# Plain stores of the shared output and a shifted loop start: a gated-expert block on one Trainium2 core

## The chip, the core and the metric

The kernel runs on one core of a Trainium2 chip. The metric is the device time of one execution in microseconds (us). Matmuls run on TensorE (PE); VectorE (DVE), ScalarE (ACT) and GpSimd (POOL) do the elementwise work; SyncE (SP) issues nearly all transfers, and each engine runs its own instruction stream, kept in step by semaphores.

## The reference

Eight rows (sequences) of 512 tokens by 256 channels go through two layers, both with a residual:

```python
# layer 0: routed experts (top 2 of 8 per row) and one shared expert
rw = softmax(cond_8); w, sel = top_k(rw, 2); w = w / w.sum(-1)
mlp(x, g, u, d) = (gelu(x @ g) * (x @ u)) @ d        # 256 -> 1024 -> 256
x = x + sum_k w[b, k] * mlp(x, skill[sel[b, k]]) + mlp(x, shared)
# layer 1: a linear map plus LoRA experts weighted by cond_8
x = x + x @ W_base.T + b_base + 2 * sum_e cond_8[b, e] * (x @ As[e].T) @ Bs[e].T
```

All of it is float32.

## The kernel before

Every float32 operand is split in two parts of a format that TensorE multiplies in one pass: ScalarE rounds it ("hi", `take_hi`, L1201), VectorE subtracts to get the rest ("lo", `take_lo`, L1586). A product is three passes, hi*hi, hi*lo and lo*hi (`product`, L851 to L855), so TensorE's work is one long list of 128x128 by 512 (or 256) matmuls. Larger products are done with seven block products in place of eight; the sums of weight blocks that this needs are made by GpSimd (four operations, L806 to L811), split by ScalarE and VectorE, and the results are put together by VectorE (L1648, L1650, L1885, L1900, L1902) and GpSimd (`c22`, L739, and `ex_c22`, L820).

**Shared part (0 to about 255 us).** Four quarters `q` of two rows each; each has four units `u`, a unit being one fourth of the inner channels: gate and up products, then the down products of the unit before, added up in four PSUM banks `acc[0..1][0..1]`. When a quarter is done, ScalarE copies `acc[0]` (`acc0_to_stage`, L1308) and VectorE `acc[1]` (`acc1_to_stage`, L1689) to `stage`. In HBM there are two scratch tensors of rows, `xt_dram` and `base_dram`; SyncE stores the transposed tokens to both (`store_xt`, L503). GpSimd then issues two transfers that add `stage` to `base_dram` (`add_shared`, L706 and L709) and signal `sh_stored`. `stage` is also where GpSimd makes its sums of tokens (`t_a`, `t_b`, L770 and L782; `t_c` lies in `post`), the sums of the first rows (`sums_of_x`, L746) and, in rows, the sums of weights (`s_tmp`), so each of these waits for `sh_stored`. In the unit loop GpSimd's order is: c22 of gate, t_a, c22 of up, t_b, t_c.

**Rows (about 255 us to the end).** Eight rows `b` of K = 16 steps `k`, two experts of eight chunks. Steps come in pairs; pairs 1, 3, 5, 6, 7 (`SEVEN`, in row 0 without 1) are done as seven products on the last even step, pairs 0, 2, 4 as whole products, with VectorE's multiply of gate and up at L1976. In step 1 of row b+1 VectorE adds `base` and the PSUM sums of row b (`layer1_sum`, L1842), and in step 5 TensorE does layer 1 of row b (`layer1`, 24 matmuls in PSUM banks called ps_acc). `base` is loaded by SyncE once per row (L629 for row 0, L659 later) when layer 1 of the row before has let it go. Each engine has its own loop over rows 1 to 6, two rows an iteration, three iterations (GpSimd: one row an iteration). TensorE's loop starts at step `TURN_STEP` = 6 of row 1; VectorE's, ScalarE's and SyncE's start at step 0 of row 1 (VectorE L2018), so they turn at the starts of rows 3 and 5.

In row 0, GpSimd first does `add_shared(Q - 1)`, waits for `sh_stored` = 16 * B, and makes the weight sums of pair 3 (`sums_of_weights(b, 1, True)`, L828); ScalarE splits them in step 5 and VectorE too (`SUMS_FIRST`), VectorE behind its multiply of step 5; TensorE needs them in the second of the seven products of step 6.

**Start.** TensorE does 13 filling transposes of the identity (L975), turns the first row (L969), does 5 more fillers (L981), and begins the first gate (`first_gate`, L874 to L883).

## Time and profile before

| | |
|---|---|
| median of 3 runs | 806.21 us (804.76 to 808.38) |
| profiled execution | 809.66 us, its span 807.8 us |
| TensorE busy | 793.7 us, 98% of the span, 4282 matmuls |
| VectorE busy | 655.3 us, 81% |
| ScalarE busy | 498.3 us, 62% |
| GpSimd busy | 313.4 us, 39% |
| granted TensorE clock, mean | 0.995 |
| moved by DMA | 108.82 MB |

The span is from the first to the last instruction of the profiled execution; the time of an execution has some 1.9 us around it. Ends of matmuls are modelled, so a stretch of matmuls that is drawn longer than the same list elsewhere is also a loss, beside the gaps. "Idle before, releaser" is the time for which an engine stood still before an instruction and what ended it; "issue" there means that the profile shows nothing that it waited for.

### The profile page before, as it was taken

The numbers are of one execution on the slowest core, as the hardware profiler recorded it, in microseconds if no ns is written. First come the engines' busy times: TensorE is split into PE (matmuls) and PEld (weight loads), VectorE is DVE, ScalarE is ACT, GpSimd is POOL, SyncE is SP. The second block draws the span as 40 slices with busy tenths as digits, with TensorE's granted clock in tenths as the row PEclk, the third lists the DMA queues.
The fourth block names the chain that finished last, engine by engine and source line by source line (L and its number), as shares of the span: only waits on it lengthen the run. The fifth ranks groups of instructions, "written<-read, shape, count | busy, mean of one in ns | idle before, by whom it ended". The sixth has DMA issues, their size and how long they took to land.

```text
span 807.8 us, 14151 instructions
## 1 busy us (share of the span) xinstructions
PE 793.7 (98%) x4282; PEld 690.3 (85%) x4282; DVE 655.3 (81%) x872; ACT 498.3 (62%) x808; POOL 313.4 (39%) x308
## 2 busy tenths in 40 slices
PE   9999999999999899999999999999999999999998
PEld 8888878878878789889888978988988998898897
DVE  4866888988987578978987977897888789789777
ACT  5554554555664466666766766676766767667663
POOL 1531431521530245435444424633445352454341
PEclk9999999999999999999999999999999999999999
DMA  7456806708516632743463256265246526623400
GB/s 221 115 169 196 194 2 193 173 0 272 121 51 183 170 118 79 234 133 117 138 212 95 84 192 169 78 205 159 87 130 206 135 69 205 169 78 101 109 1 27
DMA packets 139894, 108.82 MB, mean 135 GB/s; under 512 B 63040, under 2 KB 131392, under 8 KB 139840
## 3 DMA queue, kind: packets, MB, share of 16 engines
q1 hardware_dynamic: 136384, 104.00, 41.9%
q0 software_dynamic: 3456, 4.19, 3.3%
q8 instruction: 22, 0.36, 0.2%
q14 instruction: 32, 0.26, 0.1%
HBM read 79.34 MB, written 28.84 MB: 134 GB/s over the span
## 4 chain that ended last, share of the span: by engine, by line
PE 87%; DVE 4%; issue 3%; POOL 2%; DMA 2%; ACT 1%; DVEq 0%; ACTq 0%; POOLq 0%
PE ps_ring L853 54%; PE ps_acc L853 31%; DMA base_scratch<-stage 2%; DVE inner_lo L1586 1%; DVE xc L1586 1%; DVE post L1675 1%; POOL stage L807 1%; PE ps_ring L975 0%; ACT wide L1201 0%; PE ps_acc L1072 0%; PE ps_acc L969 0%; DVE post L1976 0%; POOL stage L806 0%; POOL stage L811 0%; ACT inner_hi L1201 0%
## 5 line engine op out<-in xcount | busy, mean ns | idle before, releaser
L853 PE MATMUL ps_ring<-xc,wide 128*128 128x512 f32 (+1 forms) x1854 | 386.8, 357 | 3.0 <-DVE post L1648 3.0
L853 PEld LDWEIGHTS ps_ring<-xc,wide 128*128 128x128 f32 x1854 | 317.5, 189 | 56.7 <-DVE post L1648 4.7
L1201 ACT CAST inner_hi<-post 128x512 fp32r<-128x512 f32 x192 | 116.3, 621 | 97.8 <-DVE post L1976 30.7
L853 PE MATMUL ps_acc<-inner_hi,wide 128*128 128x512 f32 x504 | 166.3, 390 | 0.0
L1586 DVE TENSOR_TENSOR inner_lo<-post,inner_hi 128x512 fp32r<-128x512 f32 (+1 forms) x145 | 137.2, 955 | 3.0 <-ACT inner_hi L1201 2.6
L1204 ACT ACTIVATE post<-post 128x256 f32<-128x256 f32 (+1 forms) x114 | 62.2, 558 | 98.2 <-DVE post L1900 69.7
L820 POOL TENSOR_TENSOR post<-post 128x256 f32<-128x256 f32 x78 | 82.0, 1072 | 95.6 <-ACT post L1453 95.6
L853 PEld LDWEIGHTS ps_acc<-inner_hi,wide 128*128 128x128 f32 x504 | 94.8, 188 | 18.9
L853 PE MATMUL ps_acc<-inner_lo,wide 128*128 128x512 f32 x252 | 98.5, 391 | 0.0
L853 PE MATMUL ps_ring<-xc 128*128 128x256 f32 x576 | 80.7, 287 | 3.7 <-DVE xc L1586 3.6
L853 PE MATMUL ps_acc<-inner_hi,sh_dn 128*128 128x512 f32 x256 | 83.9, 389 | 0.0
L1204 ACT ACTIVATE post<-ps_ring 128x512 f32<-128x512 f32 (+1 forms) x117 | 61.6, 529 | 30.9 <-PE ps_ring L853 25.4
L853 PEld LDWEIGHTS ps_ring<-xc 128*128 128x128 f32 x576 | 75.2, 196 | 4.1 <-DVE xc L1586 3.8
L806 POOL TENSOR_TENSOR stage<-xbuf 128x256 f32<-128x256 f32 x24 | 19.7, 822 | 143.2 <-DVE xc L1586 131.8
L1586 DVE TENSOR_TENSOR wide<-raw,wide 128x1536 fp32r<-128x1536 f32 (+4 forms) x38 | 58.0, 1526 | 20.3 <-ACT wide L1201 19.7
L739 POOL TENSOR_TENSOR post<-post 128x512 f32<-128x512 f32 x24 | 34.2, 1424 | 97.9 <-DVE post L1650 97.9
L1863 DVE SCALAR_TENSOR_TENSOR post<-post,coef_now 128x256 f32<-128x256 f32 x78 | 51.9, 666 | 18.7 <-ACT post L1204 17.8
L1976 DVE SCALAR_TENSOR_TENSOR post<-post,coef_now,ps_ring 128x512 f32<-128x512 f32 x50 | 37.3, 746 | 31.9 <-PE ps_ring L853 23.2
L1586 DVE TENSOR_TENSOR xc<-stage,xc 128x1024 fp32r<-128x1024 f32 (+1 forms) x50 | 60.2, 1209 | 3.5 <-ACT xc L1201 3.5
L853 PEld LDWEIGHTS ps_acc<-inner_hi,sh_dn 128*128 128x128 f32 x256 | 48.0, 188 | 10.0
L853 PEld LDWEIGHTS ps_acc<-inner_lo,wide 128*128 128x128 f32 x252 | 47.5, 188 | 8.4
L1201 ACT CAST wide<-raw 128x1536 fp32r<-128x1536 f32 (+4 forms) x40 | 48.9, 1222 | 8.9 <-DMA raw<-in_L_cond_shared_up_dram 6.0
(130 smaller groups left out, 1074.8 us busy)
## 6 DMA issues: line engine op xcount, KB each, us to landing
rights_scratch<-xc SPq DMA_DIRECT2D x6, 1792.0 KB, 11.3
raw<-n_L_cond_skill_gate_dram SPq DMA_DIRECT2D x32, 256.0 KB, 2.8
raw<-in_L_cond_skill_up_dram SPq DMA_DIRECT2D x32, 256.0 KB, 3.4
raw<-n_L_cond_skill_down_dram SPq DMA_DIRECT2D x32, 256.0 KB, 3.8
xbuf<-n_L_cond_skill_gate_dram SPq DMA_DIRECT2D x32, 256.0 KB, 2.7
xbuf<-in_L_cond_skill_up_dram SPq DMA_DIRECT2D x32, 256.0 KB, 3.2
xbuf<-n_L_cond_skill_down_dram SPq DMA_DIRECT2D x32, 256.0 KB, 3.5
xt_scratch<-xbuf SPq DMA_DIRECT2D x8, 512.0 KB, 3.4
```

The lines of the kernel that those rows point to most:

```text
L739: G.tensor_tensor((g_t if part == GATE else i_t)[3], v57, u1, ALU.add).then_inc(c22_done, 1)
L806: G.tensor_tensor(s1, a21, a22, ALU.add).then_inc(ex_s1_made, 1)
L807: G.tensor_tensor(s3, a11, a21, ALU.subtract)
L820: last = G.tensor_tensor(ex_v[:, half], ex_v[:, half], ex_u1[:, half], ALU.add)
L853: last = pe.matmul(dst, left_[a], right_[b], start=start and n == 0, stop=stop and n == len(PASSES) - 1, skip_group_check=adds)
L1201: return nc.scalar.copy(dst, src)
L1204: return nc.scalar.activation(dst, src, ACT.Gelu_apprx_tanh)
L1586: return V.tensor_tensor(dst, src, hi.bitcast(F32), ALU.subtract)
L1675: V.tensor_tensor(i_t[t], g_t[t], i_t[t], ALU.mult).then_inc(sh_mul, 1)
L1863: V.scalar_tensor_tensor(out=to, in0=g, scalar=coef_now[:, par, s:s + 1], in1=up, op0=ALU.mult, op1=ALU.mult).then_inc(ex_mul, 1)
L1976: V.scalar_tensor_tensor(out=inner[k % 2], in0=gelu[k % 2], scalar=coef_now[:, par, s:s + 1], in1=ring[2 + k % 2][:], op0=ALU.mult, op1=AL ...
```

## The change

- `base_dram` is gone. `store_xt` stores the tokens once. A new `sh_dram` takes the shared output alone, by plain stores that SyncE issues (`store_shared`), for quarters 0 and 1 behind the first token store of the next iteration, for quarter 2 before the last store of rights, for quarter 3 in row 0 behind the loads of the layer 1 constants.
- SyncE loads `base` from `sh_dram`. GpSimd adds the tokens to it in SBUF with one accumulating transfer a row (`add_tokens`), issued behind `ex_c22(b, 1)`, which is the c22 of step 6. It signals `base_ready`, and VectorE's `layer1_sum` waits for that.
- VectorE's loop begins at step 8 (`DVE_TURN_STEP`) of row 1: `row` takes a range of steps; the turns lie in the middle of rows 3 and 5.
- The 5 filling transposes behind the first turning are left out.
- Counts of `xt_stored` are halved; a few waits on events of long before are added, and three operations in `layer1_constants` are cut in halves.

```diff
@@ -62,6 +62,8 @@
     X1_LO_STEP = 4
     TURN_STEP = 6
+
+    DVE_TURN_STEP = 8
@@ -124,8 +126,7 @@
         last_bank = [acc[1][0], acc[1][1], ring[0], ring[1]]
         xt_dram = nc.dram_tensor("xt_scratch", [B, P, HC * S], F32, kind="Internal").ap()
-
-        base_dram = nc.dram_tensor("base_scratch", [B, P, HC * S], F32, kind="Internal").ap()
+        sh_dram = nc.dram_tensor("sh_scratch", [B, P, HC * S], F32, kind="Internal").ap()
         rights_dram = nc.dram_tensor("rights_scratch", [B - 1, P, 2 * NP * HS], F32, kind="Internal").ap()
@@ -390,6 +391,7 @@
         t_made = sem("t_made")
         v_done = sem("v_done")
         c22_done = sem("c22_done")
+        base_ready = sem("base_ready")
         x_rows = x.rearrange("b (p t) h -> b p t h", t=TT)
         out_rows = out.rearrange("b (p t) h -> b p t h", t=TT)
@@ -498,9 +500,22 @@
                     sp.wait_ge(xt0_in, 2 * r + 2)
                 else:
                     sp.wait_ge(xt_in, 4 * (qn - 1) + 2 * r + 2)
-
-                for to in (xt_dram, base_dram):
-                    sp.dma_start(to[2 * qn + r], xbuf[:, r * 2 * S:(r + 1) * 2 * S]).then_inc(xt_stored[r], 16)
+                sp.dma_start(xt_dram[2 * qn + r], xbuf[:, r * 2 * S:(r + 1) * 2 * S]).then_inc(xt_stored[r], 16)
+
+            def shared_place(q, n):
+                if q == 0:
+                    return sh_dram[n], stage[:, n, :]
+
+                return (sh_dram[2 * q:2 * q + 2].rearrange("r p (m h t) -> p m h r t", m=HC, h=2)[:, :, n],
+                        stage[:, n, :].rearrange("p (m r t) -> p m r t", m=HC, r=2))
+
+            def store_shared(q):
+                sp.wait_ge(acc0_out, 2 * (q + 1))
+                to, what = shared_place(q, 0)
+                sp.dma_start(to, what).then_inc(sh_stored, 16)
+                sp.wait_ge(acc1_out, 2 * (q + 1))
+                to, what = shared_place(q, 1)
+                sp.dma_start(to, what).then_inc(sh_stored, 16)
             def store_rights(q):
@@ -571,6 +586,8 @@
                     sp.wait_ge(xt_in, 4 * q + 2)
                     load_x_blocks(2 * qn + 1, x_blk)
                 store_xt(qn, 0)
+                if q > 0:
+                    store_shared(q - 1)
                 if qn < Q - 1:
                     sp.wait_ge(xt_in, 4 * q + (2 if q == 0 else 4))
                     load_x_blocks(2 * qn + 2, x_blk)
@@ -590,11 +607,12 @@
             sp.wait_ge(right_ready, rights(Q - 1, NP))
             sp.wait_ge(right_hi, rights(Q - 1, NP))
             for r in range(2):
-                sp.wait_ge(xt_stored[r], 32 * Q)
+                sp.wait_ge(xt_stored[r], 16 * Q)
             sp.wait_ge(xt_in, 4 * (Q - 1))
             sp.dma_start(xf_first, xt_dram[0]).then_inc(x0_landed, 16)
             gate0, up0, down0 = first_expert()
             fill_slot(2, gate0, up0, down0)
+            store_shared(Q - 2)
             store_rights(Q - 1)
             sp.wait_ge(x_ready, 1)
@@ -626,7 +644,7 @@
                 if first:
                     sp.wait_ge(sh_mul, 4 * NU)
                     sp.wait_ge(sh_stored, 16 * (B - 2))
-                    sp.dma_start(base, base_dram[b]).then_inc(base_landed, 16)
+                    sp.dma_start(base, sh_dram[b]).then_inc(base_landed, 16)
                     sp.wait_ge(sh_inner_hi, 4 * NU)
                     sp.wait_ge(sh_inner_ready, 4 * NU)
@@ -639,6 +657,7 @@
                             .then_inc(layer1_landed, 16)
                     sp.dma_start(w_nat, w_base.rearrange("(c p) h -> p c h", p=P))\
                         .then_inc(layer1_landed, 16)
+                    store_shared(Q - 1)
                     sp.wait_ge(sums_stored, 16)
                     sp.wait_ge(sh_down_done, 2 * NU)
@@ -656,7 +675,7 @@
                     sp.wait_ge(x1_ready, b)
                     sp.wait_ge(sh_stored, 16 * B)
-                    sp.dma_start(base, base_dram[b]).then_inc(base_landed, 16)
+                    sp.dma_start(base, sh_dram[b]).then_inc(base_landed, 16)
                     load_routed(b, 1, range(3, 4))
                     if not last:
                         load_routed(b + 1, 0, range(0, 1))
@@ -690,24 +709,6 @@
             G.affine_select(out=ident[:], in_=ident[:], compare_op=ALU.not_equal, fill=1.0,
                             base=0, pattern=[[-1, P]], channel_multiplier=1).then_inc(ident_ready, 1)
-            def shared_place(q, n):
-                if q == 0:
-                    return base_dram[n], stage[:, n, :]
-
-                return (base_dram[2 * q:2 * q + 2].rearrange("r p (m h t) -> p m h r t", m=HC, h=2)[:, :, n],
-                        stage[:, n, :].rearrange("p (m r t) -> p m r t", m=HC, r=2))
-
-            def add_shared(q):
-
-                for r in range(2):
-                    pool.wait_ge(xt_stored[r], 32 * (q + 1))
-                pool.wait_ge(acc0_out, 2 * (q + 1))
-                to, what = shared_place(q, 0)
-                pool.dma_start(to, what, accum_op=ALU.add).then_inc(sh_stored, 16)
-                pool.wait_ge(acc1_out, 2 * (q + 1))
-                to, what = shared_place(q, 1)
-                pool.dma_start(to, what, accum_op=ALU.add).then_inc(sh_stored, 16)
-
             def left_sums(j):
                 v = raw[j % 2][:, 0:4 * PW].rearrange("p (g c i) -> p g c i", g=2, c=HC)
@@ -782,8 +783,6 @@
                     G.tensor_tensor(both(t_b), xh(1, 1), xh(0, 1), ALU.subtract).then_inc(t_made, 1)
                     pool.wait_ge(t_made, 4 * q + 1)
                     G.tensor_tensor(both(t_c), xh(1, 1), both(t_a), ALU.subtract).then_inc(t_made, 1)
-                if q > 0 and j == 0:
-                    add_shared(q - 1)
                 if u < PAIRS - 1:
                     pool.wait_ge(sh_landed[u + 1], 32)
@@ -820,9 +819,15 @@
                     last = G.tensor_tensor(ex_v[:, half], ex_v[:, half], ex_u1[:, half], ALU.add)
                 last.then_inc(ex_c22_done, 1)
+            def add_tokens(b):
+
+                pool.wait_ge(base_landed, b * 16 + 16)
+                pool.dma_start(base, xt_dram[b], accum_op=ALU.add).then_inc(base_ready, 16)
+
             def row(b, first, last):
                 if first:
-                    add_shared(Q - 1)
+                    for r in range(2):
+                        pool.wait_ge(xt_stored[r], 16 * Q)
                     pool.wait_ge(sh_stored, 16 * B)
                     sums_of_weights(b, 1, True)
@@ -831,6 +836,7 @@
                     ex_c22(b, 0)
                 sums_of_weights(b, 2)
                 ex_c22(b, 1)
+                add_tokens(b)
                 sums_of_weights(b, 3)
                 sums_of_weights(b, 4)
                 ex_c22(b, 2)
@@ -947,8 +953,8 @@
             def shared_down_part(u, p):
                 q, j = divmod(u, PAIRS)
-                if q == 0 and p == 0:
-                    pe.wait_ge(sh_dn_ready, j + 1)
+                if q == 0 or j == 0:
+                    pe.wait_ge(sh_dn_ready, j + 1 if q == 0 else PAIRS)
                 if u == 0 and p == 0:
                     pe.wait_ge(xt0_in, 4)
@@ -976,9 +982,6 @@
             pe.wait_ge(x_landed[0], 16)
             for c in range(HC):
                 turn(acc[0][c], x_nat, c)
-
-            for _ in range(5):
-                pe.transpose(ring[3][:, 0:P], ident[:], ident[:])
             first_unit()
             for u in range(1, NU):
@@ -1613,7 +1616,7 @@
                     dve.wait_ge(right_hi, rights(qn - 1, NP))
                     dve.wait_ge(right_ready, rights(qn - 1, NP))
-                dve.wait_ge(xt_stored[r], 32 * qn)
+                dve.wait_ge(xt_stored[r], 16 * qn)
                 blk = x_blk1 if qn == 1 and r == 1 else x_blk
                 for c in range(HC):
                     V.transpose(xt(r, c), blk[:, c, :]).then_inc(xt_in, 1)
@@ -1679,6 +1682,8 @@
                 take_lo(inner_s[1][:, t, :], i_t[t], inner_s[0][:, t, :]).then_inc(sh_inner_ready, 1)
             def acc1_to_stage(q):
+                if q > 0:
+                    dve.wait_ge(acc0_out, 2 * q)
                 dve.wait_ge(sh_down_done, 2 * PAIRS * (q + 1))
                 if q == 0:
@@ -1822,18 +1827,25 @@
             inner_part(NU - 1, 3)
             def layer1_constants():
+
+                dve.wait_ge(acc0_out, 2 * Q)
+                dve.wait_ge(layer1_landed, 6 * 16)
                 dve.wait_ge(a_hi, 1)
-                take_lo(a_s[1], a_nat, a_s[0]).then_inc(a_ready, 1)
+                for half in (slice(0, P), slice(P, H)):
+                    last = take_lo(a_s[1][:, half], a_nat[:, half], a_s[0][:, half])
+                last.then_inc(a_ready, 1)
                 dve.wait_ge(turned_w, 1)
                 V.tensor_copy(b_t[:], ps_misc[1][:, 0:H]).then_inc(b_t_done, 1)
-                V.tensor_copy(w_id[:], ps_misc[0][:]).then_inc(w_turned, 1)
+                for c in range(HC):
+                    last = V.tensor_copy(w_id[:, c * H:(c + 1) * H], ps_misc[0][:, c * H:(c + 1) * H])
+                last.then_inc(w_turned, 1)
                 dve.wait_ge(w_turned, 1)
                 for c in range(HC):
                     d = w_id[:, c * H + c * P:c * H + (c + 1) * P]
                     V.tensor_tensor(d, d, ident[:], ALU.add).then_inc(w_id_done, 1)
             def layer1_sum(b):
-                dve.wait_ge(base_landed, b * 16 + 16)
+                dve.wait_ge(base_ready, b * 16 + 16)
                 for m in range(HC):
                     if m < HC - 1:
                         dve.wait_ge(sum_done, b + 1)
@@ -1909,7 +1921,7 @@
                 ex_inner(par, s, inner[1].rearrange("p (t n) -> p t n", t=2),
                          gelu[1].rearrange("p (t n) -> p t n", t=2), ex_c2[:, :, HS:S])
-            def row(b, par, first, last):
+            def row(b, par, first, last, steps=range(K)):
                 split_at = SPLIT_FIRST if first else SPLIT_LATER
                 sums_at = SUMS_FIRST if first else SUMS_LATER
@@ -1935,7 +1947,7 @@
                     cols = slice(0, 2 * S) if first else slice(HS, S)
                     take_lo(x_cur(1 - par, 1)[:, cols], xf[:, cols], x_cur(1 - par, 0)[:, cols]).then_inc(x_ready, 1)
-                for k in range(K):
+                for k in steps:
                     s = k // IC
                     if k // 2 in sevens_of(first):
                         if k % 2 == 0:
@@ -2015,11 +2027,13 @@
                     .then_inc(x1_ready, 1)
             row(0, 0, True, False)
+            row(1, 1, False, False, range(DVE_TURN_STEP))
             with dve.Fori(0, (B - 2) // 2) as i:
-                row(i * 2 + 1, 1, False, False)
+                row(i * 2 + 1, 1, False, False, range(DVE_TURN_STEP, K))
                 row(i * 2 + 2, 0, False, False)
-            row(B - 1, 1, False, True)
-            dve.wait_ge(base_landed, B * 16)
+                row(i * 2 + 3, 1, False, False, range(DVE_TURN_STEP))
+            row(B - 1, 1, False, True, range(DVE_TURN_STEP, K))
+            dve.wait_ge(base_ready, B * 16)
             for c in range(HC):
                 if c == 0:
```

## Rows read from the trace of the kernel before

**Rows 1.** Waits of TensorE: us in total, times, longest.

```profile
PE ps_ring L853 <- DVE post L1648: 3.0, 4, 1.6
```

**Rows 2.** Timeline of TensorE: start, us, line, tiles, count, idle before.

```profile
103.92 0.97 PE L853 MATMUL ps_ring<-xc,wide 128*128 128x512 f32 x3 [1.61 <-DVE post L1648]
...
164.82 0.96 PE L853 MATMUL ps_ring<-xc,wide 128*128 128x512 f32 x3 [0.76 <-DVE post L1648]
...
279.79 0.87 PE L853 MATMUL ps_ring<-xc,wide 128*128 128x256 f32 x6
284.24 3.85 PE L853 MATMUL ps_ring<-xc 128*128 128x256 f32 x18 [3.58 <-DVE xc L1586]
...
290.08 0.40 PE L853 MATMUL ps_acc<-inner_hi,wide 128*128 128x512 f32 x1
```

**Rows 3.** Chain that ended last, in time order: start, us, what.

```profile
265.69 13.16 DMA base_scratch<-stage
...
414.11 5.44 PE ps_acc L853 x24
...
484.65 5.44 PE ps_acc L853 x24
490.09 5.03 PE ps_ring L853 x42
...
551.49 5.44 PE ps_acc L853 x24
...
619.57 5.44 PE ps_acc L853 x24
```

**Rows 4.** Window behind the wait of row 0: PE busy, PEclk, DMA share.

```profile
284.20:286.00 1.80, 1.76 (x8) 0.50 0.99 324
```

**Rows 5.** GpSimd: the tile base_scratch (ns min/median/max), then its timeline.

```profile
L709 POOL DMA_DIRECT2D base_scratch<-stage x4: 1182/1921/1992, 85.8 to 265.7; - x4
...
98.08 1.74 POOL L782 TENSOR_TENSOR stage<-xbuf 128x512 f32<-128x512 f32 x1
...
493.73 1.76 POOL L820 TENSOR_TENSOR post<-post 128x256 f32<-128x256 f32 x2 [2.85 <-ACT post L1453]
502.66 0.88 POOL L806 TENSOR_TENSOR stage<-xbuf 128x256 f32<-128x256 f32 x1 [7.16 <-DVE xc L1586]
```

**Rows 6.** Timeline of VectorE.

```profile
98.59 1.77 DVE L1675 TENSOR_TENSOR post<-post 128x512 f32<-128x512 f32 x1
...
101.99 0.68 DVE L1675 TENSOR_TENSOR post<-post 128x512 f32<-128x512 f32 x1
...
278.69 0.75 DVE L1976 SCALAR_TENSOR_TENSOR post<-post,coef_now,ps_ring 128x512 f32<-128x512 f32 x1 [1.68 <-PE ps_ring L853]
...
465.60 0.75 DVE L1976 SCALAR_TENSOR_TENSOR post<-post,coef_now,ps_ring 128x512 f32<-128x512 f32 x1 [1.71 <-PE ps_ring L853]
...
469.92 0.75 DVE L1976 SCALAR_TENSOR_TENSOR post<-post,coef_now,ps_ring 128x512 f32<-128x512 f32 x1 [2.05 <-issue]
...
500.70 0.75 DVE L1976 SCALAR_TENSOR_TENSOR post<-post,coef_now,ps_ring 128x512 f32<-128x512 f32 x1
...
504.16 0.75 DVE L1976 SCALAR_TENSOR_TENSOR post<-post,coef_now,ps_ring 128x512 f32<-128x512 f32 x1 [1.22 <-PE ps_ring L853]
```

**Rows 7.** Chain at the start of the kernel.

```profile
4.56 1.71 PE ps_acc L969 x8
6.26 1.07 PE ps_ring L981 x5
...
11.65 0.87 PE ps_acc L969 x8
```

**Rows 8.** Page, DMA issues: count, KB each, us to landing.

```profile
rights_scratch<-xc SPq DMA_DIRECT2D x6, 1792.0 KB, 11.3
...
xt_scratch<-xbuf SPq DMA_DIRECT2D x8, 512.0 KB, 3.4
```

**Rows 9.** Timeline of SyncE's queue, the base load of row 3.

```profile
484.08 0.34 SPq L659 DMA_DIRECT2D post<-base_scratch  x1
```

## The prediction

> **What bounds the kernel now.** I read the waits of TensorE first, then its own timeline around them, the chain of work in order of time for the distances between equal pieces, and last VectorE and GpSimd beside each gap. TensorE is busy 98% of the span, so anything that does not take a gap or an instruction from TensorE is worth nothing. The reader is to see that the gaps are few and that each has one owner [rows 1, 2]:
>
> - Four waits of 3.0 us together for VectorE's L1648 (the sum v57 of a shared matrix). The two longest, 1.61 and 0.76 us, stand in the second unit of the second and of the third quarter [rows 1, 2].
> - One of 3.58 us for the lo half of the weight sums, in step 6 of row 0 [rows 2]. Its real price is more: these seven products run from 279.79 to the next down product at 290.08, 10.29 us, where the same piece takes 5.03 elsewhere [rows 2, 3]. That is 5.26 us: the wait and a slow stretch behind it, in which the granted clock is 0.50 (1.2 of 2.4 GHz) [rows 4].
> - Something at the start of rows 3 and 5. The layer 1 blocks (24 matmuls, 5.44 us) lie 66.84 us apart where no loop of VectorE turns between them (484.65 to 551.49), but 70.54 (414.11 to 484.65) and 68.08 (551.49 to 619.57) where one does [rows 3]. That is 3.70 + 1.24 = 4.94 us for two turns. VectorE stands still there twice per turn: 1.71 us before the first multiply behind the branch and 2.05 us, put down to "issue", before the next [rows 6].
>
> **The change part by part.** The sum is made against the profiled execution, 809.66 us (span 807.8 and 1.9 around it); the median of the runs shown is 806.21, 3.4 less.
>
> *Fewer filling transposes.* Five of them take 1.07 us at 6.26, straight ahead of the first matmuls, and TensorE then goes on without a gap [rows 7]. If the first operands are there at 6.26 all of it is won. But eight turning transposes took 1.71 us before this point and 0.87 us after it [rows 7]: the array was at half speed, and what runs first in place of the fillers runs at half speed too. Two bounds, 0 (the operands come just in time) and 1.07; I take half, 0.5, since half the fillers' time would then be real work at half speed.
>
> *Plain stores of the shared output, quarters 0 to 2.* Before, GpSimd issued an accumulating transfer (1.2 to 2.0 us of GpSimd for the second of each pair [rows 5]), and its next sum t_a waited until that had landed. So t_b and t_c of the next unit came late, t_b at 98.08 [rows 5]. There they meet VectorE: a multiply with two operands in SBUF takes 1.77 us at 98.59 beside GpSimd's 1.74 us sum, and 0.68 at 101.99 with GpSimd at rest [rows 5, 6]. The two take turns. Three VectorE operations are slowed by 1.1 us each before the L1648 that TensorE waits for. Now SyncE stores from its own queue; a plain 512 KB store lands 3.4 us after issue, the last accumulating one took 13.16 [rows 3, 8]. t_a is then done before the two sums VectorE waits for, and one of three collisions is left, perhaps two. In the second quarter VectorE is early by some 1.6 us, which just takes the 1.61; the third has 0.76 to give; the last two waits (0.6 together) lie by the sums of x, of which only the first waits for a store: 0.2. Sum 2.4, bounds 1.0 (two collisions left) and 3.0. What is moved on SyncE: each pair of stores stands between a token store and the loads of the row pair after it, which wait for a transpose that VectorE makes after it has copied acc1 out. So nothing in the queue comes later, save the last store of rights (some 17 us later), which is first waited for in row 0.
>
> *The last shared store, row 0.* Before, the second accumulating transfer took 13.16 us from 265.69 [rows 3]; GpSimd's sums, ScalarE's hi, VectorE's lo followed, then TensorE. Plain stores of 1 KB pieces ran at 1792 KB in 11.3 us [rows 8], which gives 3.2 us for each of the two, 6.5 for both from about 264.3: landed near 271. GpSimd's four sums (about 3 us) are done by 274. What is late next is VectorE's own place in its program: the lo of these sums stands behind the multiply of step 5, which starts at 278.69 and takes 0.75 [rows 6]. 279.4 + 1.2 = 280.6, and TensorE asks for it at 279.79 + 0.72 = 280.5. So about 0.1 is left of the wait, no slow clock behind it, and 5.0 of 5.26 is won. Bounds: 3.0 (the stores land at 275 behind other traffic, a 1.5 us wait with a bit of slow clock) and 5.26. On SyncE the rights load, the tokens and the slot 2 weights behind the stores leave 2 to 3 us later (it waits for acc1), all for steps 8 and later. The slot 3 load behind them waits for the sums and leaves 8 us earlier.
>
> *Tokens added in SBUF.* GpSimd issues one accumulating transfer a row behind its second c22. It costs 1.2 to 2.0 us of issue [rows 5]. In row 3 that c22 starts at 493.73 (1.76 us for the pair) and the next sums start at 502.66 after 7.16 us of rest [rows 5], so it is hidden five times over. The base that it waits for is issued at 484.08 [rows 9], 11 us before. The result is wanted at step 1 of the next row, some 40 us later. 0 us; if the cover were gone it would be 1 to 2 us in each of 8 rows. The bytes moved stay the same (one store less in the shared part, one transfer more in the rows), so I take nothing for the memory.
>
> *VectorE's loop at step 8.* Its two turns leave the starts of rows 3 and 5 and go to the middle of them. The 4.94 us go, and a new stall comes. The place is not idle: the first multiply of step 8 starts at 500.70 with no rest before it [rows 6]. With the standstill seen at the branch, between 1.3 and 1.7 us, it starts at about 502.2; the lo of the weight sums and GpSimd's sums hang on it. VectorE rests 1.22 us before its next multiply, at 504.16 [rows 6], and I estimate about as much again from there to the next sum of a seven. A first standstill is just absorbed; a second one like the 2.05 would be late by about 1 us, partly through GpSimd. I take 0.6 a turn, bounds 0 and 2.5 (as bad as before). Won: 4.94 - 1.2 = 3.7.
>
 By that rule alone the gain is what the new place can hide, and it might be nothing; that is the first rival below. The trace agrees with the rule as far as it goes: both standstills follow L2018's branch.
>
> *Small ones.* Two more instructions in the layer 1 constants (0.1 us beside rest of VectorE), three waits long fulfilled: 0.
>
> Sum: 0.5 + 2.4 + 5.0 + 3.7 = 11.6. The profiled execution would take 798.1, the median 794.6. The slow clock behind the turn at row 3 (3.70 against 1.24) may be rarer in the unprofiled runs, which are 3.4 us faster; I give back 0.4 and say 795.0.
>
> **The rivals.**
> 1. The turn costs at step 8 what it cost at step 0: 795.0 + 3.7 = 798.7. For it: 500.70 has no rest before it, and the weight sums of two pairs go through GpSimd right after. Against: the rest before 504.16, which takes up most of one standstill.
> 2. The stores don't come early enough in row 0, or VectorE's lo of step 5 is late by more than 0.1, so that TensorE stops for 1 to 2 us and its clock falls: 2 to 3 us of the 5.0 are lost, 797.5. For it: the weights of slot 2, the tokens and the rights are loaded in the same stretch. Against: 3 us between the sums and their use.
> 3. The other side: GpSimd is held in every row. It issues the accumulating transfer in program order, and if issue and wait together hold it for more than the 7.16 us of rest [rows 5], the sums of the seventh pairs come late, and every microsecond more is lost in all seven later rows. It decides from about 8 us; to eat the 11.6 us of gain it needs 1.7 us a row more, some 10 us in all, and then the time is 807; at 11 us, 813. Against: issue costs at most 2 us and the base has 11 us to land.
> 4. The change takes the named waits away but others stood right behind them (the third quarter's, row 0's later sevens), so that half is won: 801.
>
> **How the numbers follow.** Forecast as said (792 to 798): 0.58. Rival 1: 0.14. Rival 2: 0.10. Rival 4: 0.11. Rival 3: 0.07, of which 0.02 ends within 0.5%. About 0.5% (4 us) is what a measurement of this kernel can tell from no change. Faster needs less than 802.2: the first three cases, and most of rival 4, 0.88; within 0.5%: 0.07; slower: 0.05. The lower end takes every bound at its best, 806.2 - 0.9 of 1.07 - 3.0 - 5.26 - 4.94 = 792, with one below for what I have not seen: 791. The upper end is rival 4's 801.
>
> **What would show it.** In the profile after: the 3.58 us wait gone and 5.0 to 5.3 us between start and end of row 0's first seven products; L1648's longest wait under 0.5 us; layer 1 blocks 66.8 to 68 us apart in all rows; VectorE's standstill now before the multiply of step 8 in rows 3 and 5; GpSimd's new transfer between the second c22 and the next sums. Wrong would be: equal distances of about 68 to 70 us at rows 3 to 4 and 5 to 6 (rival 1), a slow clock in row 0 (rival 2), GpSimd's sums after the new transfer later than 9 us behind c22 in every row (rival 3).

## The result, and the profile after

The changed kernel takes 799.82 us (median of 6 runs, 799.54 to 800.66), the kernel before 805.62 in the same comparison (804.73 to 808.55): ratio 0.992, 95% interval 0.9901 to 0.9938. That is 5.8 us faster where 11 were forecast; the time lies inside the stated range (791 to 801), near its upper end.

| | before | after |
|---|---|---|
| median of the runs | 805.62 us | 799.82 us |
| profiled execution | 809.66 us, span 807.8 | 800.2 us, span 798.5 |
| TensorE busy | 793.7 us | 790.7 us |
| VectorE busy | 655.3 us | 653.6 us |
| GpSimd busy | 313.4 us | 311.5 us |
| granted clock, mean | 0.995 | 1.0 |

The two profiled spans are 9.3 us apart, the medians 5.8. A second profile of the kernel before (span 804.1, the last experiment) shows why: the first was longer than is usual for it. Both are used below. The experiments ran on different chips, where the kernel before has medians of 805.4 to 806.5 us; a difference of some tenths between medians of two experiments says little by itself.

TensorE's waits in the changed kernel (us in total, times, longest). The waits for L1648 and for the weight sums of row 0 [rows 1, 2] are gone. The wait for a ScalarE copy, which had two cases of 0.3 us together, now stands five times with 2.7 us:

```profile
PE ps_ring L859 <- ACT ps_ring L1442: 2.7, 5, 1.3
```

Row 0's first seven products on TensorE now run from 275.83 to 281.09, 5.26 us where they took 10.29 [rows 2]:

```profile
275.83 0.87 PE L859 MATMUL ps_ring<-xc,wide 128*128 128x256 f32 x6
276.67 2.42 PE L859 MATMUL ps_ring<-xc 128*128 128x256 f32 x18
...
281.09 0.40 PE L859 MATMUL ps_acc<-inner_hi,wide 128*128 128x512 f32 x1
```

The last two stores on SyncE, then GpSimd's first sum, then VectorE. The sums begin at 265.49, in place of 278.94, and are done long before VectorE comes to split them; its lo (275.40) stands right behind its multiply of step 5, as forecast:

```profile
260.12 0.63 SPq L515 DMA_DIRECT2D sh_scratch<-stage  x1
261.46 0.62 SPq L518 DMA_DIRECT2D sh_scratch<-stage  x1
```

```profile
265.49 0.73 POOL L805 TENSOR_TENSOR stage<-xbuf 128x256 f32<-128x256 f32 x1 [19.99 <-DMA sh_scratch<-stage]
```

```profile
274.74 0.75 DVE L1988 SCALAR_TENSOR_TENSOR post<-post,coef_now,ps_ring 128x512 f32<-128x512 f32 x1 [1.24 <-PE ps_ring L859]
275.40 1.22 DVE L1589 TENSOR_TENSOR xc<-stage,xc 128x1024 fp32r<-128x1024 f32 x1
```

In the second unit of the second quarter one collision of VectorE and GpSimd and part of a second are left: VectorE's 1.27 and 1.78 us beside GpSimd's 1.74 at 96.51, and then 0.68, where three operations were slowed before [rows 5, 6]. VectorE, then GpSimd:

```profile
95.83 1.27 DVE L1678 TENSOR_TENSOR post<-post 128x512 f32<-128x512 f32 x1
97.02 1.78 DVE L1589 TENSOR_TENSOR inner_lo<-post,inner_hi 128x512 fp32r<-128x512 f32 x1
98.73 0.68 DVE L1678 TENSOR_TENSOR post<-post 128x512 f32<-128x512 f32 x1
```

```profile
95.26 1.29 POOL L783 TENSOR_TENSOR stage<-xbuf 128x512 f32<-128x512 f32 x1
96.51 1.74 POOL L785 TENSOR_TENSOR post<-xbuf,stage 128x512 f32<-128x512 f32 x1
```

The layer 1 blocks in the chain of work. They lie 66.84 us apart, but 69.33 (472.06 to 541.39) and 68.79 (608.23 to 677.02) in the rows where VectorE's loop turns, now in their middle. The two turns cost 2.49 + 1.95 = 4.44 us, where they cost 4.94 before [rows 3]:

```profile
405.22 5.44 PE ps_acc L859 x24
...
472.06 5.44 PE ps_acc L859 x24
...
541.39 5.44 PE ps_acc L859 x24
...
608.23 5.44 PE ps_acc L859 x24
...
677.02 5.44 PE ps_acc L859 x24
```

What happens at such a turn, on VectorE, GpSimd, ScalarE and TensorE of row 3. VectorE stands still for 2.75 us ahead of the multiply of step 8 ("issue": the profile names nothing that it waited for); GpSimd's next sums start after 9.12 us of rest; ScalarE's copy L1442, which in its program stands behind the hi of those sums, is late, and TensorE waits 1.29 us for it:

```profile
486.90 1.22 DVE L1589 TENSOR_TENSOR inner_lo<-post,inner_hi 128x1024 fp32r<-128x1024 f32 x1
490.87 0.75 DVE L1988 SCALAR_TENSOR_TENSOR post<-post,coef_now,ps_ring 128x512 f32<-128x512 f32 x1 [2.75 <-issue]
491.53 1.22 DVE L1589 TENSOR_TENSOR xc<-stage,xc 128x1024 fp32r<-128x1024 f32 x1
```

```profile
481.14 1.76 POOL L819 TENSOR_TENSOR post<-post 128x256 f32<-128x256 f32 x2 [2.84 <-ACT post L1456]
482.85 0.88 POOL L825 DMA_DIRECT2D post<-xt_scratch  x1
492.84 0.87 POOL L805 TENSOR_TENSOR stage<-xbuf 128x256 f32<-128x256 f32 x1 [9.12 <-DVE xc L1589]
...
495.19 0.74 POOL L810 TENSOR_TENSOR stage<-xbuf,stage 128x256 f32<-128x256 f32 x1
```

```profile
496.04 1.05 ACT L1204 CAST xc<-stage 128x1024 fp32r<-128x1024 f32 x1 [1.22 <-POOL stage L810]
496.99 0.58 ACT L1442 COPY ps_ring<-ps_ring 128x512 f32<-128x512 f32 x1
```

```profile
497.62 0.98 PE L859 MATMUL ps_ring<-sh_dn,xc 128*128 128x256 f32 x6 [1.29 <-ACT ps_ring L1442]
```

The row of GpSimd at 482.85 is the new accumulating transfer: 0.88 us of issue, in GpSimd's rest, as forecast. VectorE never waits for it.

### The profile page after: what moved, and what is told of

It reads as the page before. It is cut to its first block, busy times and chain, and to the rows that moved or that the text cites. A ratio compares the mean times of both kernels' runs of the same rounds, so it can differ in the third digit from the quotient of the medians.

```text
span 798.5 us, 14174 instructions
## 1 busy us (share of the span) xinstructions
PE 790.7 (99%) x4277; PEld 687.0 (86%) x4277; DVE 653.6 (82%) x874; ACT 497.6 (62%) x808; POOL 311.5 (39%) x308
## 4 chain that ended last, share of the span: by engine, by line
PE 89%; issue 4%; POOL 4%; DVE 1%; ACT 1%; POOLq 0%; DVEq 0%; ACTq 0%
PE ps_ring L859 55%; PE ps_acc L859 32%; POOL post L819 1%; POOL stage L805 1%; POOL stage L810 1%; POOL stage L808 1%; POOL stage L806 1%; DVE xc L1589 0%; PE ps_ring L981 0%; PE ps_acc L1075 0%; PE ps_acc L975 0%; DVE wide L1589 0%; PE ps_ring L880 0%; PE ps_ring L885 0%; PE ps_ring L889 0%
## 5 line engine op out<-in xcount | busy, mean ns | idle before, releaser
L740 POOL TENSOR_TENSOR post<-post 128x512 f32<-128x512 f32 x24 | 31.0, 1293 | 127.3 <-DVE post L1653 127.3
L859 PE MATMUL ps_ring<-xc 128*128 128x256 f32 x576 | 79.0, 283 | 0.2 <-ACT ps_ring L1442 0.2
L859 PEld LDWEIGHTS ps_ring<-xc 128*128 128x128 f32 x576 | 73.4, 192 | 0.6 <-ACT ps_ring L1442 0.4
L1589 DVE TENSOR_TENSOR wide<-xbuf,wide 128x1280 fp32r<-128x1280 f32 (+1 forms) x32 | 49.7, 1553 | 5.4 <-POOL stage L810 5.4
```

The source lines that it names most:

```text
L740: G.tensor_tensor((g_t if part == GATE else i_t)[3], v57, u1, ALU.add).then_inc(c22_done, 1)
L859: last = pe.matmul(dst, left_[a], right_[b], start=start and n == 0, stop=stop and n == len(PASSES) - 1, skip_group_check=adds)
L1589: return V.tensor_tensor(dst, src, hi.bitcast(F32), ALU.subtract)
```

## The experiments

Each kernel is told by its edit and by the excess of the two blocks with a turn over 66.84 us, read from its chain of work.

One more view is needed. The DMA queues of the profile hold two queues of kind "instruction"; what moves in them is program, not data. In the one called q14 single packets of 8 KB appear, and at a turn with a standstill one of them begins about where VectorE stops. In this document it is called the fetch packet. The queue carries no engine's name. That the packets at the turns are VectorE's is read from this: they come and go when nothing but VectorE's loop is edited, and VectorE goes on at a nearly fixed time behind them (table behind experiment 9).

**1. The stores alone.** The changed kernel with VectorE's loop at step 0 and the fillers put back.

```diff
-            row(1, 1, False, False, range(DVE_TURN_STEP))
             with dve.Fori(0, (B - 2) // 2) as i:
-                row(i * 2 + 1, 1, False, False, range(DVE_TURN_STEP, K))
+                row(i * 2 + 1, 1, False, False)
                 row(i * 2 + 2, 0, False, False)
-                row(i * 2 + 3, 1, False, False, range(DVE_TURN_STEP))
-            row(B - 1, 1, False, True, range(DVE_TURN_STEP, K))
+            row(B - 1, 1, False, True)
...
+            for _ in range(5):
+                pe.transpose(ring[3][:, 0:P], ident[:], ident[:])
```

> The change without its loop start at step 8 and with the five fillers put back: only the plain stores and the tokens added in SBUF. Theory (the stores give the gain, the loop's new place next to nothing): 1.00 us or less slower than the whole change, about 800.7 (before 805.6); in its profile TensorE waits again at the starts of rows 3 and 5, layer 1 blocks there about 68 to 70.5 us apart, row 0's first seven products 5.1 us long. Rival (the loop's place gives 3.7 and the stores little): 803.5 to 804.

Measured: 801.71 us (800.72 to 802.23), before 805.73, ratio 0.994 [0.9922, 0.9958]. Excess 2.72 and 2.94 us. The stores give about 4 of the 5.8 us; the loop's place and the fillers together about 1.9, more than the 1.00 at most of the theory. The rival is out. (That the loop at step 0 costs 5.7 us here and less in the kernel before was not expected; see the end.)

**2. The loop at step 8 alone**, in the kernel before.

```diff
-            with dve.Fori(0, (B - 2) // 2) as i:
-                row(i * 2 + 1, 1, False, False)
-                row(i * 2 + 2, 0, False, False)
-            row(B - 1, 1, False, True)
+            row(1, 1, False, False, range(DVE_TURN_STEP))
+            with dve.Fori(0, (B - 2) // 2) as i:
+                row(i * 2 + 1, 1, False, False, range(DVE_TURN_STEP, K))
+                row(i * 2 + 2, 0, False, False)
+                row(i * 2 + 3, 1, False, False, range(DVE_TURN_STEP))
+            row(B - 1, 1, False, True, range(DVE_TURN_STEP, K))
```

> The kernel before with only VectorE's loop begun at step 8. Theory (a turn costs at step 8 what it cost at step 0): layer 1 blocks over the turns 68.5 to 69.5 us apart, the time within 1 us of before (805.6). Rival 1 (the new place is cheap, and what makes it dear in the whole change is the accumulating transfer in flight at the turn): blocks under 67.5 us apart and 3 to 4 us faster, 802. Here the transfer isn't there.

Measured: 806.73 us (804.37 to 808.49), before 805.73, ratio 1.0004 [0.9991, 1.0018]: no difference. But the excesses are 1.29 and 1.16 us, half of what the same place costs in the whole change, and the standstills are 1.72 and 1.58 us. On VectorE of this kernel:

```profile
497.58 0.75 DVE L1977 SCALAR_TENSOR_TENSOR post<-post,coef_now,ps_ring 128x512 f32<-128x512 f32 x1 [1.72 <-issue]
```

So the theory holds for the time and fails in its blocks (68.13 and 68.00 us apart, where 68.5 was the least), rival 1 is out with its 802, and something in the whole change lengthens the standstill. The transfer in flight is one candidate, the place of the branch target in the program another.

**3. Without the five fillers alone**, in the kernel before.

```diff
-            for _ in range(5):
-                pe.transpose(ring[3][:, 0:P], ident[:], ident[:])
```

> The kernel before without the five filling transposes. Theory (they were replaced by real work at half speed): 0.3 to 0.5 us faster, 805.2. Rival (all 1.07 us won): 804.5. Rival (a later wait takes it back): no difference.

Measured: 806.6 us (804.94 to 807.72), ratio 1.0006 [0.9993, 1.0019]. Nothing is to be seen; the kernel before spreads over 3 us and more. Experiment 5 asks again.

**4. The loop at step 6**, in the whole change.

```diff
-    DVE_TURN_STEP = 8
+    DVE_TURN_STEP = 6
```

> The whole change with VectorE's loop begun at step 6 in place of 8. There VectorE rests 2.08 us before the first sum of the seven products (row 3 of the changed kernel). Theory (a turn holds VectorE for 2.8 to 4 us from the branch on wherever it is, and only the rest at that place hides it): the standstill hides, layer 1 blocks over the turns 66.8 to 67.6 apart, 3 to 4.4 us faster than the whole change: 795.5 to 797. Rival (a turn costs TensorE about 2 us wherever it stands): 799.8.

Measured: 795.26 us (794.86 to 795.5), ratio to before 0.9861 [0.9842, 0.988]: 4.6 us faster than the changed kernel. No excess in any block. On VectorE the first sum of step 6 comes behind 2.08 us of waiting for TensorE, as it does without a turn (1.97 in experiment 7):

```profile
475.88 1.25 DVE L1868 STREAM_TRANSPOSE stage<-post 128x1024 f32<-128x1024 f32 x1 [0.28 <-ACT post L1410]
479.20 0.69 DVE L1897 TENSOR_TENSOR post<-ps_ring,post 128x512 f32<-128x512 f32 x1 [2.08 <-PE ps_ring L859]
```

```profile
471.47 5.44 PE ps_acc L859 x24
...
538.31 5.44 PE ps_acc L859 x24
...
605.15 5.44 PE ps_acc L859 x24
```

The time is what the theory said, but its reason, a standstill hidden inside the rest, is not what the trace shows. There is no fetch packet at these turns to be hidden. The whole changed kernel has 32 packets in q14, this one 22:

```profile
q14 instruction: 32, 0.26, 0.1%
```

```profile
q14 instruction: 22, 0.18, 0.1%
```

The ten that are missing are those of the rows with the loop: between 435 and 715 us the changed kernel has ten packets in q14, and this one none at all. So at step 6 VectorE's branch, like those of the other engines, finds its instructions without a fetch. That its length would have fitted into the rest was not tried. The rival, 2 us a turn wherever it stands, is out.

**5. The fillers again**, on the steadier kernel with the loop at step 6.

```diff
+            for _ in range(5):
+                pe.transpose(ring[3][:, 0:P], ident[:], ident[:])
```

> The loop at step 6 (795.26) with the five fillers put back. Theory (real work at half speed in their place): 0.3 to 0.5 us slower, 795.7. Rival (all of the 1.07 us is won by leaving them out): 796.3. Rival (no difference, since the clock rises at its own time and the operands come just then): 795.3.

Measured: 795.35 us (795.09 to 795.63) against 795.26 (794.86 to 795.5): no difference that stands clear of the spread of 0.6 us. The 1.07 us of the first rival are out; of the theory's 0.3 to 0.5 nothing is seen.

**6. No token transfer**, loop at step 8.

```diff
-                pool.dma_start(base, xt_dram[b], accum_op=ALU.add).then_inc(base_ready, 16)
...
-                dve.wait_ge(base_ready, b * 16 + 16)
+                dve.wait_ge(base_landed, b * 16 + 16)
...
-            dve.wait_ge(base_ready, B * 16)
+            dve.wait_ge(base_landed, B * 16)
```

> The whole change (loop at step 8), with the accumulating transfer that adds the tokens left out (the output lacks the tokens there) and VectorE waiting for the base alone. Theory (the transfer in flight is what makes the fetch at the turn longer: 2.75 and 2.24 us against 1.72 and 1.58 in the kernel before with the loop at step 8): standstills of 1.6 to 1.8 us again, 1.2 us a turn, 2 us faster, 797.8. Rival (the place of the branch target in the program makes it longer): standstills and time as in the whole change, 799.8.

Measured: 797.75 us (797.57 to 797.96), 2.1 us less than the changed kernel. Standstills 1.86 and 1.55 us, excess 1.61 and 1.27. The expectation was met to 0.1 us, in part by luck: the excesses are smaller by 1.56 us together (4.44 to 2.88), and in the two profiles another 0.77 is a later start (first 36 matmuls in a row at 16.30 and at 15.53), which the transfer has no part in. VectorE at the turn, and the windows around it (PEclk, then the share of the DMA engines' time, then GB/s) in this kernel and in the changed one:

```profile
489.21 0.75 DVE L1988 SCALAR_TENSOR_TENSOR post<-post,coef_now,ps_ring 128x512 f32<-128x512 f32 x1 [1.86 <-issue]
```

```profile
486.00:488.00 2.00, 1.35 (x2) 1.00 0.20 56
488.00:490.00 2.00, 0.79 (x2) 1.00 0.85 252
```

```profile
486.00:488.00 2.00, 2.00 (x2) 1.00 1.07 207
488.00:490.00 2.00, 0.12 (x1) 1.00 1.09 277
```

With the transfer the 16 DMA engines are full from 486 to 490. Without it they are nearly idle from 485.5 to 487.5 (0.10 and less), and busy with other loads only behind that (0.71 and more). The fetch packet shows what this does. In the window 486.8 to 487 of this kernel, and then in the window 488.7 to 490.9 of the changed one (packets, MB, share of the DMA engines' time):

```profile
q14 instruction: 1, 0.01, 18.0%
```

```profile
q14 instruction: 1, 0.01, 0.9%
```

VectorE's last operation before the turn starts at 486.13 here and the packet at 486.87, 0.74 us later. In the changed kernel they start at 486.90 and 488.72, 1.82 us apart; the last packet of the token transfer had started at 488.30. So the packet does not take longer (0.31 us there, 0.57 here): it starts later, about when the transfer is through.

**7. VectorE without a loop.**

```diff
-            row(1, 1, False, False, range(DVE_TURN_STEP))
-            with dve.Fori(0, (B - 2) // 2) as i:
...
+            for b in range(1, B - 1):
+                row(b, b % 2, False, False)
+            row(B - 1, 1, False, True)
```

> The whole change with VectorE's rows written out, without a loop on VectorE. Theory (the turn is the whole cost at step 8, and step 6 hides it all): layer 1 blocks 66.8 us apart everywhere, 795.2 as with the loop at step 6. Rival (something else than the branch is in step 8, or step 6 leaves something unhidden): more than 0.5 us away from 795.26.

Measured: 795.07 us (794.8 to 795.13), all blocks 66.84 us apart. So the loop's turn is the whole price of step 8 (4.75 us by the medians, 4.44 by the excesses), and at step 6 at most 0.2 us is left of it. Written out, the rows have four packets in q14 between 435 and 715 us, and at none of them does VectorE stand still for over 0.3 us with nothing named: these fetches cost next to nothing.

**8. The loop at step 4.**

```diff
-    DVE_TURN_STEP = 8
+    DVE_TURN_STEP = 4
```

> The whole change with VectorE's loop begun at step 4, where VectorE rests 1.39 us before the multiply. Theory (what the rest doesn't hide is seen by TensorE, if VectorE has no more time up to the next use): a standstill 1.4 to 1.7 us longer than the rest alone would be is mostly hidden by the rest, TensorE loses 0 to 1 us a turn, 795.3 to 797. Rival (any whole-product step costs 2 us a turn): 799.8.

Measured: 794.91 us (794.85 to 795.04), ratio to before 0.9854 [0.9833, 0.9875], no excess. The rest ahead of the multiply is there as without a turn: 1.03 us, for TensorE, where the kernel without a loop has 1.02. The rival, that any whole-product step costs 2 us, is out. The theory's cover is not what did it either: a standstill of 1.55 us, the shortest seen at step 8, would have shown beyond a rest of 1.03. As at step 6, q14 has 22 packets in all and none between 435 and 715 us, so nothing was fetched at the turn.

**9. The token transfer later**, loop at step 8.

```diff
                 ex_c22(b, 1)
-                add_tokens(b)
                 sums_of_weights(b, 3)
                 sums_of_weights(b, 4)
+                add_tokens(b)
                 ex_c22(b, 2)
```

> The whole change (loop at step 8), with GpSimd's accumulating transfer issued two groups of weight sums later in every row, behind the fourth instead of ahead of the third, so that it is not in flight at the turn; nothing is left out. Theory (the transfer in flight makes the fetch longer): standstills of 1.6 to 1.9 us at the turn as without the transfer, 797.8. Rival (the transfer costs its 2 us somewhere in any case, or delays the c22 behind it): 799.8 or more.

Measured: 802.68 us (802.17 to 803.18), slower than the changed kernel by 2.9. The standstills are short (1.62 and 1.74 us) with the transfer in the kernel but not in flight. The first:

```profile
491.55 0.75 DVE L1988 SCALAR_TENSOR_TENSOR post<-post,coef_now,ps_ring 128x512 f32<-128x512 f32 x1 [1.62 <-issue]
```

So the theory's mechanism holds, and its time does not. What it missed is GpSimd's own queue: the 0.87 us of issue now stand ahead of a c22 that ScalarE and TensorE wait for, and in the rows without a turn the blocks lie 67.25 to 67.39 us apart, 0.4 to 0.55 more than 66.84. (The turns themselves add 1.6 and 1.7 us to that.) TensorE's wait in row 3 is 0.95 us:

```profile
502.56 0.74 POOL L810 TENSOR_TENSOR stage<-xbuf,stage 128x256 f32<-128x256 f32 x1
503.24 0.87 POOL L825 DMA_DIRECT2D post<-xt_scratch  x1
503.85 1.73 POOL L819 TENSOR_TENSOR post<-post 128x256 f32<-128x256 f32 x2
```

```profile
507.34 0.98 PE L859 MATMUL ps_ring<-sh_dn,xc 128*128 128x256 f32 x6 [0.95 <-ACT ps_ring L1442]
```

The rival, a cost that appears somewhere in any case, was right for this place.

The fetch packets at the turns, from the traces (us; row 3, then row 5; for the loop at step 0 the range of the first packets of the turns in experiments 1, 3, 11 and the kernel before):

| kernel | from the start of VectorE's last operation to the packet | from the packet to VectorE's next operation | standstill |
|---|---|---|---|
| loop at step 0 | 0.70 to 0.93 | 2.16 to 2.30 | 1.67 to 1.89 |
| 2, step 8, no token transfer | 0.73, 0.71 | 2.21, 2.08 | 1.72, 1.58 |
| 6, step 8, transfer left out | 0.74, 0.71 | 2.34, 2.07 | 1.86, 1.55 |
| 9, step 8, transfer later | 0.74, 0.71 | 2.11, 2.25 | 1.62, 1.74 |
| changed kernel, step 8 | 1.82, 1.33 | 2.15, 2.13 | 2.75, 2.24 |
| 4, 5, 8, 10, steps 4 and 6 | no packet | | none named |

**10. Plain stores issued by GpSimd**, loop at step 6: `store_shared` moved from SyncE's program into GpSimd's, at the places of `add_shared`.

```diff
-                if q > 0:
-                    store_shared(q - 1)              # SyncE, also behind q = Q - 2 and Q - 1
...
+                pool.dma_start(to, what).then_inc(sh_stored, 16)
...
+                if q > 0 and j == 0:
+                    store_shared(q - 1)              # GpSimd's unit loop
...
+                    store_shared(Q - 1)              # GpSimd's row 0
```

> The loop at step 6, with the shared output stored by plain transfers, but issued by GpSimd at the places of the kernel before. It tells what of the gain in the shared part and row 0 comes from dropping the accumulation, and what from SyncE's queue. Theory (the accumulation is the slow thing): landing 4 to 6 us after issue, no wait in row 0, 0 to 1 us slower than 795.26. Rival (GpSimd's queue is slow as such, the last store lands 9 to 13 us after issue): row 0's wait of 3 us with its slow clock is back, 799 to 800.

Measured: 795.72 us (795.5 to 796.03), 0.5 more than with SyncE. The last store is on the chain with 8.55 us, where the accumulating one had 13.16 [rows 3], and TensorE waits 0.69 us for row 0's sums. The theory's time holds; its landing of 4 to 6 us doesn't. Dropping the accumulation is most of the gain in row 0, SyncE's queue adds the last 0.7 (the stretch over row 0 is 85.54 us here and 84.82 with SyncE):

```profile
260.91 8.55 DMA sh_scratch<-stage
```

```profile
276.55 2.42 PE L858 MATMUL ps_ring<-xc 128*128 128x256 f32 x18 [0.69 <-DVE xc L1588]
```

**11. The kernel before again**, one profile, no edit.

> The kernel before, unchanged, for one more profile of it. Theory (what varies in it from run to run is how the array's clock falls behind its waits of 1.6 us and more): row 0's first seven products 9.5 to 11 us, layer 1 blocks over the turns between 67.8 and 70.6 apart, not the same as in the first profile. Rival (the differences between profiles of before come from the part that was changed in each kernel): the same to 0.2 us as the first.

Measured: 805.92 us, span 804.1, where the first profile had 809.66 and 807.8. Its waits and chain:

```profile
PE ps_ring L853 <- DVE xc L1586: 3.8, 1, 3.8
PE ps_ring L853 <- DVE post L1648: 1.9, 4, 0.8
PE ps_ring L853 <- DVE post L1976: 1.7, 2, 1.1
```

```profile
412.18 5.44 PE ps_acc L853 x24
...
480.81 5.44 PE ps_acc L853 x24
...
547.65 5.44 PE ps_acc L853 x24
...
615.77 5.44 PE ps_acc L853 x24
```

Excesses of the turns 1.79 and 1.28 (3.07 in sum, 4.94 in the first profile, 2.23 in that of experiment 3, whose rows are those of the kernel before). L1648 is waited for 1.9 us in all, not 3.0. So the theory holds and the rival, the same as in the first profile, is out. The start up to the first 36 matmuls in a row takes 14.1 us from the first filler in place of 15.1.

## Why the prediction was right or wrong

**Direction and range: right; the size was half.** Laid against the second profile of before (span 804.1 to 798.5, 5.6 us, close to the medians' 5.8), from the same landmarks of the chain: quarters +2.57, row 0 +5.08, the start -0.69, rows 1 to 7 -1.37.

**Row 0: right.** Forecast 5.0 of 5.26; 5.03 (10.29 to 5.26) for the seven products in the first profile, 5.08 for the stretch from the shared part's last block to row 1's layer 1 in the second. The chain was as told: stores landed by 265.5, sooner than the 271 of the estimate, and VectorE's place in its program came last. Experiment 10 says what did it: mostly that nothing is accumulated.

**Quarters: right.** Forecast 2.4; 3.6 against the first profile and 2.57 against the second. The waits for L1648 are gone altogether; one to two collisions of VectorE and GpSimd are left.

**Fewer fillers: wrong in size, and small.** Forecast 0.5, measured none (experiments 3 and 5). The start varies by 1 us from run to run: the eight turning transposes take 1.91, 1.63 and 1.04 us in the timelines of the kernel before, of experiment 11 and of experiment 8, where nothing ahead of them differs. The granted clock reads 1.00 there in all of them, so the rows don't say why.

**The loop at step 8: the step that failed.** The prediction took 4.94 us as the price of the old place and 0.6 us a turn for the new one, 3.7 won. Both ends were wrong, the second more. The new place costs 2.49 and 1.95 us (4.44 together). Of this 1.2 to 1.6 us a turn are there without the token transfer (experiments 2 and 6), and 1.56 us for both come from the transfer (2.1 by the medians), for which the prediction put 0. It had looked for a cost of that transfer on GpSimd and in the bytes moved, not in what the branch needs from the DMA engines. It also took the first standstill as 1.3 to 1.7 us, where the first profile has 1.71 and 1.87, and it allowed for a second one, which did not come at step 8. The working did name the chain that makes a standstill dear (lo of the sums, GpSimd's sums), and then counted VectorE's rests as cover. The rest behind the first lo covered nothing, since GpSimd starts its sums as soon as that lo is there: they came 2.8 us later than in the kernel without a loop, and ScalarE's copy is queued behind their hi. Rival 1 was that case; its 798.7 lies 1.1 us below the measured time.

**What the place of the loop does.** The prediction, and the theories of experiments 4 and 8, took a standstill as given at every place and asked what hides it. The traces show another thing: at steps 4 and 6 nothing is fetched. Of the prediction's sentence that moving a loop's start moves the stall and removes none of it, the second half is refuted. What makes the difference between steps 0 and 8 and steps 4 and 6 was not tried. All four loops hold the same two rows of work, so the position of the loop in the program is the likely cause; that is argued, not shown. If it is so, another step may be the good one when other code stands ahead of it. That steps 4 and 6 came out well was luck, as far as it was chosen by the rests.

The Trainium skill (Runtime: NRT & Kernel Launch, Instruction fetch mechanics) says that a taken branch to a target outside the two pages held has to wait for a fetch, and that the sequencer fetches through its own DMA queue. The trace agrees: where VectorE stands still, a packet of an instruction queue begins 2.1 to 2.3 us before it goes on; where there is no packet (steps 4 and 6), there is no standstill; and with the token transfer in flight the packet begins 0.6 to 1.1 us later. The prediction drew on the Trainium skill for the stall and not for the queue, which was the part that mattered.

**The old price was one execution's.** 4.94 us was the worst of three (4.94, 3.07, 2.23). In the first profile the second standstill of row 3 is 2.05 us (1.55 and 0.65 in the others), and behind TensorE's wait the granted clock is 0.50 (1.2 of 2.4 GHz) from 472 to 475 us, where it stays at 1.00 in experiment 11. 4 us of slowness of the profiled execution were subtracted as if every run had them; the give-back of 0.4 was too small.

**Rivals.** GpSimd held in every row (3) and row 0 only half won (2) did not come. Rival 3's mechanism, with a price of about 0.5 us a row, appeared in experiment 9, when the transfer was put where GpSimd has no rest. Rival 4's 801 was near the time, but nothing stood right behind the waits that went; the loss was a new one.

**A faster version.** With VectorE's loop at step 4 or 6 the changed kernel takes 794.9 to 795.3 us, 1.4% below before and 0.6% below the change as made.

## What to carry to other kernels

The turn of a loop is not free, and not always dear. Look in the DMA queues of the profile whether an instruction packet stands at the turn. If one does, try other places for the loop's start: here two of four made the packet and the whole cost go away, and only the trace told why. If it can't be made to go away, keep large transfers out of flight at that moment, and look through every engine behind the stall to the next one that has no rest. And before a stall is counted as gain, see in a second profile whether it is always that long.

## What was not expected of the hardware

- The accumulating 512 KB store in 1 KB pieces took 13.0 to 13.6 us in four profiles, the plain one from GpSimd's queue 8.55, all at the same place of the program. From SyncE's queue the last one there was issued at 261.46 and had landed by 265.49, 4.0 us, and none took over 6.1 in the changed kernel and in those of experiments 1, 4, 6 and 9.
- With the loop at step 0 a turn costs 2.72 and 2.94 us in the kernel with the new stores (experiment 1). In the kernel before it costs 3.70 and 1.24 in the first profile and 1.79 and 1.28 in the second, and 1.01 and 1.22 in experiment 3. The second standstill is there 2.22 and 2.52 us long and stands one instruction earlier, ahead of the lo of the sums in place of the second multiply. It belongs to a fetch too: with the loop at step 0 a second packet in q14 begins 3.3 to 4.6 us behind the first, and in all eight turns VectorE goes on 1.8 to 2.0 us behind it. So the late packet sets how long it stands still; in the worst turn, row 3 of the first profile, it began last (4.6 us). Why it was late there, and why it is needed one instruction earlier in experiment 1, was not tried.
